# Choosing the experts: router logits multiplied in row pieces, partly inside the layer norm, and a search on shifted logits

## What is computed

```python
logits = x @ Wr + br
probs = jax.nn.softmax(logits, axis=-1)
top_w, top_idx = jax.lax.top_k(probs, 1)
...
sel = jnp.take_along_axis(y, top_idx[:, :, None], axis=1)[:, 0]
out = sel * top_w
```

```python
logits = x @ gate_w
scores = jax.nn.softmax(logits, axis=-1)
topk_w, topk_idx = jax.lax.top_k(scores, K)
...
routed = jnp.einsum('teh,ehd,te->td', g, w_down, comb)
shared = jax.nn.silu(x @ sw_gate) * (x @ sw_up) @ sw_down
```

## Time and profile before

| | |
|---|---|
| median of three runs | 2199.68 us (2199.32 to 2202.53) |
| profiled execution | 2207.23 us |
| its span in the profile | 2205.4 us |
| PE busy in the span | 1831.6 us (83%) |
| DVE busy | 1119.1 us (51%) |
| ACT busy | 735.0 us (33%) |
| POOL busy | 491.5 us (22%) |

### The profile page before, as it was taken

The page is one execution under the profiler, slowest core; times in us unless marked ns, Lnnn a source line. Parts: engine busy times, 40 slices in busy tenths (PEclk is TensorE's granted clock), DMA queues, the critical chain, the costliest instruction groups (busy, mean ns, idle before and its releaser), DMA issues.

```text
span 2205.4 us, 32805 instructions
## 1 busy us (share of the span) xinstructions
PE 1831.6 (83%) x10372; PEld 1021.5 (46%) x10377; DVE 1119.1 (51%) x2293; ACT 735.0 (33%) x1421; POOL 491.5 (22%) x840
## 2 busy tenths in 40 slices
PE   7899999999399995749999487699468999976992
PEld 4344444443256653535666255376243444444751
DVE  6688888882322216641222456143357888452423
ACT  3277777774011110111111001022033766610210
POOL 2222222221300005530000501500442222133022
PEclk9599999997699996769999697799787999987996
DMA  4241111124100002010000400233222221002322
GB/s 118 68 131 38 38 39 38 38 102 147 45 21 20 24 22 86 1 35 27 21 21 22 155 14 5 88 95 103 62 80 56 38 37 21 2 30 82 101 89 76
DMA packets 97290, 123.34 MB, mean 56 GB/s; under 512 B 19704, under 2 KB 77976, under 8 KB 96408
## 3 DMA queue, kind: packets, MB, share of 16 engines
q1 hardware_dynamic: 87960, 96.67, 15.1%
q0 software_dynamic: 9216, 25.18, 3.5%
HBM read 78.35 MB, written 42.86 MB: 55 GB/s over the span
## 4 chain that ended last, share of the span: by engine, by line
PE 66%; DVE 13%; issue 9%; another core or an unknown queue 4%; POOL 3%; DMA 2%; ACT 1%; SPq 0%; POOLq 0%; DVEq 0%; ACTq 0%
PE psum L1374 12%; PE psum L1024 8%; PE psum L1008 7%; DVE region_a L772 6%; PE psum L1395 6%; PE psum L969 5%; PE psum L1609 5%; PE psum L1581 2%; PE psum L355 2%; POOL y_norm L1269 2%; PE psum L1627 2%; PE psum L1628 2%; PE psum L1812 2%; PE psum L1384 1%
## 5 line engine op out<-in xcount | busy, mean ns | idle before, releaser
L772 DVE TENSOR_REDUCE region_a<-psum 128x1 f32<-128x640 f32 (+7 forms) x576 | 528.5, 954 | 110.2 <-PE psum L974 58.9
L876 ACT ACTIVATE region_w<-psum 128x512 f32<-128x512 f32 x864 | 465.6, 600 | 223.8 <-PE psum L1008 220.4
L1374 PE MATMUL psum<-region_w,region_a 128*128 x608 | 271.8, 600 | 1.4 <-DVE region_a L1450 1.2
L1024 PE MATMUL psum<-region_w,region_a 128*32 128x512 f32 (+3 forms) x2304 | 254.7, 516 | 0.8 <-POOL region_w L699 0.6
L969 PE MATMUL psum<-region_a,y_norm 48*128 48x512 bf16 (+7 forms) x816 | 225.3, 352 | 5.0 <-DVE region_a L772 4.1
L699 POOL TENSOR_SCALAR_AFFINE_SELECT region_w<-region_w 128x512 f32<-128x512 f32 x192 | 122.3, 637 | 459.9 <-ACT region_w L876 455.5
L1269 POOL DMA_INDIRECT y_norm<-result_rows,region_a x64 | 63.3, 989 | 714.6 <-DMA result_rows<-region_a 696.6
L1008 PE MATMUL psum<-y_norm,region_a 51*128 51x512 bf16 (+1 forms) x612 | 206.3, 401 | 6.2 <-DMA y_norm<-region_a 4.3
L1374 PEld LDWEIGHTS psum<-region_w,region_a 128*128 128x128 f32 x608 | 114.2, 193 | 132.4 <-issue 132.4
L1581 PE MATMUL psum<-y_t,region_w 128*128 128x512 f32 (+1 forms) x192 | 101.8, 686 | 73.5 <-DVE ctx L1700 55.4
L1457 DVE TENSOR_TENSOR region_a<-psum,region_a 128x512 f32<-128x512 f32 x76 | 52.7, 693 | 215.5 <-PE psum L1374 215.5
(11 more groups left out here) (189 smaller groups left out, 2605.3 us busy)
## 6 DMA issues: line engine op xcount, KB each, us to landing
region_a<-sorted_rows SPq DMA_DIRECT2D x116, 128.0 KB, 2.0
result_rows<-region_a SPq DMA_DIRECT2D x116, 128.0 KB, 1.7
y_norm<-a_q SPq DMA_DIRECT2D x132, 64.0 KB
sorted_rows<-ctx SPq DMA_DIRECT2D x1, 4992.0 KB, 16.9
y_norm<-b_q SPq DMA_DIRECT2D x36, 128.0 KB
region_w<-in_f_wg SPq DMA_DIRECT2D x1, 4096.0 KB, 13.3
region_w<-in_f_wu SPq DMA_DIRECT2D x1, 4096.0 KB, 13.6
region_w<-in_f_wd SPq DMA_DIRECT2D x1, 4096.0 KB, 14.6
```

Source lines behind the costliest of these rows:

```text
L772: dve.tensor_reduce(dst, src, AX_X, ALU.max, negate=True).then_inc(self.ring_done.sem, 1)
L876: act.activation(self.p[col % P_RING][:, :, i % 4, :], c.bank[ST_BANKS[s % 3]].rearrange("p (h t) -> p h t", h=GQ), ACT.Exp, scale=self.sc ...
L1024: mm = pe.matmul(c.bank[ACC_BANK][32 * h:32 * h + 32, P * lo:512], self.vp[slot][:, j, :], self.p[col % P_RING][:, h, lo:4, :], start=(j = ...
L1374: mm = pe.matmul(bank[:, :], self.yt[:, f, :], w[:, f, bass.ds(own * self.hidden + 512 * half, 512)], start=(f == 0), stop=(f == FT - 1))
```

## The change

- The logits of a token group are multiplied in four pieces of 128 columns, one for each tile q, which go to the partitions 32 q onward (`multiply_logits`); before, a group was one piece of 512 columns. All four token groups so have their logits side by side, group g in the columns 128 g onward.
- Groups 0 and 1 are multiplied inside the layer norm, on TensorE between the transposes of group 2 and those of group 3; groups 2 and 3 follow behind the transposes of group 3. TensorE's wait for the router's weights moves into the layer norm with them. Group 3 has an accumulator bank of its own.
- ScalarE copies the logits of groups 0 to 2 (384 columns) ahead of those of group 3 (128 columns), and TensorE transposes the first three while the last copy runs.
- The search works on the logits less their maximum. The first choice is where that is 0, and comparison and order are one instruction; the order is laid out for all tiles, so GpSimd's memsets are wider. For the second choice the first is pushed down by a large number. Softmax is not made: when the hits are out, VectorE sums the exponentials, takes the reciprocal as the first weight, and multiplies the second exponential, which ScalarE makes, with it.
- The steps for the weights come behind the hits. The buffers are rearranged and the semaphores' totals follow.

```diff
@@ LayerNorm.tensor
         for g in range(NG):
+            if g == 3 and self.early_logits:
+                self.ready(pe, 1)
+                self.early_logits(pe, 0)
+                self.early_logits(pe, 1)
             self.normed(pe, 4 * g + 3)
@@ Routing
     def gpsimd(self, pool):
         for e in range(self.e):
-            pool.memset(self.order[:, e:e + 1], float(self.e - e)).then_inc(self.orders.sem, 1)
+            pool.memset(self.order[:, :, e:e + 1], float(self.e - e)).then_inc(self.orders.sem, 1)
+
+    def multiply_logits(self, pe, g):
+        c, e = self.c, self.e
+        self.ln.ready(pe, g)
+        if g == 0:
+            self.w_loaded(pe)
+        bank = c.bank[2 if g < NG - 1 else 1]
+        for f in range(FT):
+            for q in range(4):
+                at = 512 * g + P * q
+                mm = pe.matmul(bank[32 * q:32 * q + e, P * g:P * g + P], self.w[:, f, :], c.yt[:, f, at:at + P],
+                               start=(f == 0), stop=(f == FT - 1), skip_group_check=True)
+        if g >= NG - 2:
+            mm.then_inc(self.prod.sem, 1)
 
     def tensor(self, pe):
-        c, e = self.c, self.e
-        self.w_loaded(pe)
-        self.ln.ready(pe, NG - 1)
-        for f in range(FT):
-            for g in range(NG):
-                mm = pe.matmul(c.bank[2][32 * g:32 * g + e, :], self.w[:, f, :], c.yt[:, f, 512 * g:512 * g + 512],
-                               start=(f == 0), stop=(f == FT - 1))
+        c = self.c
+        self.multiply_logits(pe, NG - 2)
+        self.multiply_logits(pe, NG - 1)
+        for g in range(NG):
+            if g in (0, NG - 1):
+                pe.wait_ge(self.logits_set.sem, self.logits_set.at(1 if g == 0 else 2))
+            mm = pe.transpose(c.bank[3][:, P * g:P * g + P], self.logits[:, P * g:P * g + P], c.identf[:, :])
         mm.then_inc(self.prod.sem, 1)
-        pe.wait_ge(self.logits_set.sem, self.logits_set.at(1))
-        for q in range(4):
-            mm = pe.transpose(c.bank[3][:, P * q:P * q + P], self.logits[:, P * q:P * q + P], c.identf[:, :])
-        mm.then_inc(self.prod.sem, 1)
 
     def scalar(self, act):
+        c, early = self.c, P * (NG - 1)
         act.wait_ge(self.prod.sem, self.prod.at(1))
-        act.activation(self.logits, self.c.bank[2][:, :], ACT.Copy).then_inc(self.logits_set.sem, 1)
+        act.activation(self.logits[:, 0:early], c.bank[2][:, 0:early], ACT.Copy).then_inc(self.logits_set.sem, 1)
+        act.wait_ge(self.prod.sem, self.prod.at(2))
+        act.activation(self.logits[:, early:512], c.bank[1][:, early:512], ACT.Copy).then_inc(self.logits_set.sem, 1)
         act.wait_ge(self.shifted.sem, self.shifted.at(1))
         act.activation(self.pr, self.z, ACT.Exp).then_inc(self.exp.sem, 1)
+        if self.top == 2:
+            act.wait_ge(self.shifted.sem, self.shifted.at(2))
+            act.activation(self.weight[1], self.second, ACT.Exp).then_inc(self.exp.sem, 1)
@@ Routing.choose
         dve.tensor_tensor(self.z, self.z, wide(self.s), ALU.subtract).then_inc(self.shifted.sem, 1)
-        dve.wait_ge(self.exp.sem, self.exp.at(1))
-        self.then(dve, dve.tensor_reduce(self.s, self.pr, AX_X, ALU.add))
-        self.then(dve, dve.reciprocal(self.rs, self.s))
-        self.then(dve, dve.tensor_tensor(self.pr, self.pr, wide(self.rs), ALU.mult))
...
+        dve.wait_ge(self.shifted.sem, self.shifted.at(1))
+        self.then(dve, dve.scalar_tensor_tensor(out=flat(self.eq), in0=flat(self.z), scalar=0.0, in1=flat(self.order),
+                                                op0=ALU.is_equal, op1=ALU.mult))
+        self.then(dve, dve.tensor_reduce(self.s, self.eq, AX_X, ALU.max))
+        if self.top == 1:
+            dve.tensor_tensor(self.hitb, self.eq, wide(self.s), ALU.is_equal).then_inc(self.hits.sem, 1)
+        else:
+            self.then(dve, dve.tensor_tensor(self.hit[0], self.eq, wide(self.s), ALU.is_equal))
+            self.then(dve, dve.scalar_tensor_tensor(out=flat(self.left), in0=flat(self.hit[0]), scalar=NEG,
+                                                    in1=flat(self.z), op0=ALU.mult, op1=ALU.add))
+            dve.tensor_reduce(self.second, self.left, AX_X, ALU.max).then_inc(self.shifted.sem, 1)
...
+            dve.tensor_tensor(self.hitb, self.hit[0], self.hit[1], ALU.add).then_inc(self.hits.sem, 1)
+        dve.wait_ge(self.exp.sem, self.exp.at(self.top))
+        self.then(dve, dve.tensor_reduce(self.total, self.pr, AX_X, ALU.add))
+        self.then(dve, dve.reciprocal(self.weight[0], self.total))
         if self.top == 2:
-            self.then(dve, dve.tensor_tensor(self.eq, self.hit[0], self.hit[1], ALU.add))
-        assert self.top <= 2
-        dve.tensor_copy(self.hitb, self.eq if self.top == 2 else self.hit[0]).then_inc(self.hits.sem, 1)
+            self.then(dve, dve.tensor_tensor(self.weight[1], self.weight[1], self.weight[0], ALU.mult))
```

## The result

The changed kernel took 2187.24 us (median of 20 runs), the kernel before 2202.97 us (20 runs): a ratio of 0.9931 with a 95% interval of 0.9917 to 0.9946, or 15.2 us less (11.9 to 18.3). The forecast was 7.2 us less. The direction is right and the time lies inside the stated range of 2186 to 2197, but outside the forecast's own 2190 to 2195, and the gain is twice the forecast.

The account below looks back on a forecast made before the run. Bound: the path to the scatter in four expert stages, with TensorE's shared matmuls covering the top-two search. Gains 2.64, 3.09, 0.62 and 0.8 us, together 7.2, take 2199.68 to 2192.5; forecast's own range 2190 to 2195, eight in ten 2186 to 2197.

Parts of the forecast that it names:

- What bounds the kernel: Expert stages: every routed step ahead of the scatter sets the end; in top-two stages TensorE's shared matmuls cover the search.
- That the gain is kept: Behind the scatter's start distances stay at 25.1 and 51 us, so an earlier scatter is kept to the end.
- The pieces: Logits: 128-column pieces still run four at a time, 0.85 us per token group at half clock, 0.43 at full.
- The early block is not put into idle time: Layer norm: multiplying groups 0 and 1 takes 2.0 us, moving the start of group 3's transposes from T0 + 1.9 to 3.9.
- The search: VectorE: six steps, 1.5 us, gain 1.84 us in each routed stage; nothing in top-two stages, where shared matmuls end later.
- The clock's moment: TensorE's rise from 1.2 to 2.4 GHz was assumed to come at the same moments as before, T0 + 8.3 or 8.5 in two stages.
- the clock rises sooner: Rival, 25%: idle gaps gone, full clock from T0 + 3.9, stage gains together 16.4 us; 2183.3 to 2190.
- Later clock: Rival, 12%: no long logits block, so the clock rises later in the top-two stages; 2194 to 2197.6.
- the slower case: Rival, 5%: half clock for the whole of the shared matmuls, 13.4 us in both top-two stages; 2204.0.
- Pieces that pass singly: Rival, 8%: pieces pass one or two at a time, or shape changes cost more; gain gone at 0.45 us per group.

Follow-up runs that it names:

- the run with the wait: Changed kernel with all logit pieces behind the last transposes and a wait for group 3's copies, restoring TensorE's 0.9 us pause; ratio 0.9947 to the kernel before.
- the best version: Changed kernel with group 0's pieces ahead of group 2's transposes and the count behind the shared expert's first block; 2173.64 us, ratio 0.9843 to the kernel before.

## Why the prediction was right in direction and half the size

- **What bounds the kernel: right. That the gain is kept: right in the routed stages.** There the experts' first matmul comes 25.11 us after the scatter's start (598.60 - 573.49) against 25.13. In the top-two stages the distance of 51 us is no constant: that two rows agreed on it (51.10 and 50.99) was luck, since it varies by up to 4.5 us in one kernel (last section). The time and the four stretches fit a gain that is kept (15.2 and 14.64 us); stage by stage it is not shown there.
- **The pieces: right.** Group 0 and 1 took 1.82 us at half clock (562.53 to 564.35; forecast 2.0), group 3's transposes started at T0 + 3.72 (3.9), the last copy took 0.28 us (0.28), the weights were there without a wait. The pieces pass four at a time: all 32 took 3.59 us in the run with the wait, as long as the old block. The Trainium skill, "TensorEngine Tiling (Array Packing)", Key Properties, says that changing the tiling mode drains TensorE; with a tail of 0.22 us for each of the two changes the block would be an estimated 1.70 + 0.44 = 2.14 us. The trace has 1.82, so the switch costs less than a tail here.
- **The early block is not put into idle time: right.** Without it the sum was no larger (64.43 and 65.35).
- **The search: right.** 1.59 us in the first routed stage (568.35 to 569.94; forecast 1.5), covered in the top-two stages, where the count waited for the shared expert until T0 + 14.62 although the hits were out at 12.21. VectorE idled 2.62 us there even with the steps for the weights moved in.
- **The clock's moment: wrong.** This is the step that failed: "if the clock rises at the same moments as before" in the logits' part, and in the sum "at half clock until the same rise, so half is left". The rise moved from T0 + 8.3 or later to T0 + 4.2 to 6.1. The routed stages gained 1.3 and 0.9 us more than forecast, the top-two stages 3.0 and 2.35: the shared expert's first two blocks now run at full clock throughout, 1352.50 to 1359.37.
- **The forecast without the clock was near.** The run with the pause put back comes close to the world that it described: late rises, new pieces, new search. Its gains of 2.55, 2.70, 2.11 and 1.03 make 8.4 us against 7.2. It has no early block, though, and in the second and third stage its clock rose at T0 + 9.6 and 9.3 where the kernel before had none and 12.8, so the moments are not quite the same.
- **The rival "the clock rises sooner" is what happened,** at 25% rather than 50%. That 2187.24 lies inside the stated range is owed to the half of this rival that the range took in; the forecast's own part of it, 2190 to 2195, was missed. The rival's 16.4 us took the rise at T0 + 3.9; with 4.2 to 6.1 it was 14.6. Its grounds, no pauses, were the cause, as the filled pauses, the counter-test and the stages with like falls show. What I set against it was not: I read the rise at the end of one long block as a sign that the block's length brings it. That block also was the first work behind a pause of 0.88 us, and the same rows could not tell the two apart.
- **The other rivals did not occur.** Later clock: the shared matmuls ran at 1.00 in both stages. Half clock in them, the slower case: likewise. Pieces that pass singly: 1.82 us.

## What to carry to other kernels

Where TensorE waits for less than a microsecond after a longer idle time, look at the granted clock behind the wait before costing the wait at its own length: here filling pauses of 0.88 and 0.7 us gained 1.6 to 3.0 us a stage, because all that followed had run at 1.2 GHz for longer. Put pieces that are ready in front of the ones that are waited for: without the pause the same instructions took 7.2 us less up to the scatters, where the shorter search brought 3.4. A shorter step behind a cover gains nothing until the covering work is moved.

## What the runs showed of the hardware

**Useless work can pay.** Two unread matmuls in the pauses of the unchanged kernel brought a ratio of 0.9972 (0.9957 to 0.9987). What is shown is that the rise comes sooner where TensorE works on without a pause from T0. It is not shown how long a pause may be: in the changed kernel one of 0.33 us, behind the rise, did no harm.

**A distance that varies in one and the same kernel.** From the scatter's start to the experts' first transpose the two top-two stages took 51.10 and 50.99 us in the first profile of the kernel before, and 46.58 and 47.98 in the second; the changed kernel 49.46 and 50.87, then 46.54 and 46.56. I had taken 51 us for a constant. TensorE in the first top-two stage of the kernel before, the second profile:

```profile
1405.09 5.73 PE L1581 MATMUL psum<-y_t,region_w 128*96 128x512 f32 x8 [6.39 <-issue]
...
1419.26 3.58 PE L1594 MATMUL psum<-region_w,ctx 96*128 96x256 f32 x8 [4.99 <-issue]
```

and the first profile:

```profile
1403.83 6.26 PE L1581 MATMUL psum<-y_t,region_w 128*96 128x512 f32 x8 [8.74 <-issue]
...
1420.17 0.59 ACT L1660 ACTIVATE ctx<-psum 96x512 f32<-96x512 f32 x1 [24.07 <-remote]
...
1421.54 3.78 PE L1594 MATMUL psum<-region_w,ctx 96*128 96x256 f32 x8 [8.00 <-DVE ctx L1700]
```

TensorE stands still twice during the scatter, 6.39 and 4.99 us in one, 8.74 and 8.00 in the other. "issue" means that the profile shows nothing it waited for. The 8.00 us are put down to VectorE's L1700, which stands behind ScalarE's L1660; and ScalarE had stood idle 24.07 us ahead of that (20.29 in the second profile), where the profile names no instruction of this core that it waited for ("remote"). So it is not TensorE alone that stands still there. Up to 4.5 us a stage come and go between scatter and transpose, which makes 7.5 of the 10.3 us between the two spans of the kernel before (2205.4 and 2195.1); the second profile's execution took 2197.10 us, another single one on the same chip 2211.68. That is why the stages' own times tell more than spans. What the engines wait for is open, and so is whether the best version's other 9 us come from it. Its distances were 48.24 and 46.71, then 46.65 and 46.63: against the first profile of the kernel before they are 7.1 us shorter together, against the second no shorter (94.95 and 94.56), so these values do not settle it.
